# Writing out the loops over chunks of a graph network's steps, and turning a chunk's new states to rows one chunk later

## The reference

```python
h = jnp.maximum(_layernorm(x), 0.0)
# 5 times:
messages = h[col] @ W_msg.T + b_msg
agg = jax.ops.segment_sum(messages, row, num_segments=num_nodes)
gi = agg @ W_ih.T + b_ih
gh = h @ W_hh.T + b_hh
r = sigmoid(i_r + h_r); z = sigmoid(i_z + h_z); n = tanh(i_n + r * h_n)
h = (1.0 - z) * n + z * h
# at the end
return x + h
```

## Time and profile before

| | us |
|---|---|
| runs of the kernel before, median of 2 | 6251.72 (6239.28 to 6264.16) |
| the profiled execution's own time | 6248.37 |
| its span, first to last instruction | 6246.6 |
| first gather of the steps issued (the steps begin) | 1097.0 |

### The profile page before, as it was taken

How to read it: one execution, slowest core, us unless ns; L and a number is a source line. 1 busy time by engine, 2 the same in 40 slices (tenths; PEclk the granted TensorE clock), 3 DMA queues, 4 the chain that set the end, 5 groups by cost and what they waited for, 6 DMA issues and landing times.

```text
span 6246.6 us, 261732 instructions
## 1 busy us (share of the span) xinstructions
PE 4820.9 (77%) x112184; PEld 3776.4 (60%) x112185; DVE 3473.5 (56%) x6216; ACT 3188.3 (51%) x6141; POOL 236.3 (4%) x254
## 2 busy tenths in 40 slices
PE   3664777788888877778888888888788887777777
PEld 1423665666666666666666666666666666666665
DVE  6998777455555554545555555555555554444444
ACT  6202777555555554545455555555555554444444
POOL 0000000000000000000000000000000000000000
PEclk8987888999999999999999999999999999999998
DMA  2002443333333332323323233333233333333332
GB/s 71 2 1 74 163 164 159 113 99 96 101 95 104 102 93 91 102 93 97 97 92 103 92 104 97 100 102 100 95 104 95 100 103 98 97 97 97 97 97 75
DMA packets 227296, 603.16 MB, mean 97 GB/s; under 512 B 23316, under 2 KB 143425, under 8 KB 225966
## 3 DMA queue, kind: packets, MB, share of 16 engines
q1 hardware_dynamic: 217950, 566.55, 27.4%
q0 software_dynamic: 8272, 19.43, 1.3%
HBM read 467.05 MB, written 118.84 MB: 94 GB/s over the span
## 4 chain that ended last, share of the span: by engine, by line
PE 65%; issue 16%; DVE 15%; ACT 2%; DMA 1%; DVEq 1%; SPq 0%; ACTq 0%; POOL 0%
PE f_ps_c L783 21%; PE f_ps_b L769 12%; PE f_ps_a L769 11%; PE f_ps_d L729 3%; PE f_ps_d L816 3%; PE f_ps_d L810 2%; PE f_ps_d L811 2%; PE f_ps_d L812 2%; DVE f_ring L979 2%; PE f_ps_c L803 2%; PE f_ps_d L817 2%; PE f_ps_d L818 2%; PE f_ps_c L823 2%; DVE f_ring L1118 2%; DVE f_hr L1123 1%
## 5 line engine op out<-in xcount | busy, mean ns | idle before, releaser
L783 PE MATMUL f_ps_c<-f_ring 128*32 128x256 f16 x49000 | 2595.7, 281 | 242.5 <-issue 200.5
L588 ACT CAST f_ring<-f_ps_b 128x512 f16<-128x512 f32 x2082 | 1185.0, 588 | 1299.8 <-PE f_ps_b L769 1293.8
L588 ACT CAST f_ring<-f_ps_a 128x512 f16<-128x512 f32 x2083 | 1191.2, 588 | 1157.8 <-PE f_ps_a L769 1151.6
L783 PEld LDWEIGHTS f_ps_c<-f_ring 128*32 128x32 fp8e4 x49000 | 1365.1, 99 | 473.5 <-issue 386.6
L769 PE MATMUL f_ps_b<-f_hr,f_ring 128*32 128x256 f16 x24496 | 1334.9, 281 | 286.1 <-issue 285.0
L769 PE MATMUL f_ps_a<-f_hr,f_ring 128*32 128x256 f16 x24504 | 1297.8, 282 | 200.0 <-issue 190.2
L1151 DVE CAST f_ring<-f_ps_b 128x512 f16<-128x512 f32 x980 | 673.4, 687 | 1085.0 <-PE f_ps_b L769 1084.3
L1151 DVE CAST f_ring<-f_ps_a 128x512 f16<-128x512 f32 x980 | 673.4, 687 | 932.3 <-PE f_ps_a L769 931.8
L769 PEld LDWEIGHTS f_ps_b<-f_hr,f_ring 128*32 128x32 fp8e4 x24496 | 682.7, 99 | 459.8 <-issue 441.0
L769 PEld LDWEIGHTS f_ps_a<-f_hr,f_ring 128*32 128x32 fp8e4 x24504 | 676.6, 99 | 358.8 <-issue 339.3
L508 POOL DMA_INDIRECT f_ring<-fast_hrows,f_idx_tab x245 | 231.1, 943 | 5927.0 <-PE f_ps_c L793 4588.3
(11 more groups left out here) (257 smaller groups left out, 5431.1 us busy)
## 6 DMA issues: line engine op xcount, KB each, us to landing
f_ring<-fast_adj_e SPq DMA_DIRECT2D x245, 800.0 KB, 4.6
f_ring<-fast_adj_o SPq DMA_DIRECT2D x245, 800.0 KB, 6.2
fast_adj_o<-f_ring SPq DMA_DIRECT2D x49, 800.0 KB, 3.4
fast_adj_e<-f_ring SPq DMA_DIRECT2D x49, 800.0 KB, 3.4
f_ring<-fast_deg SPq DMA_DIRECT2D x245, 128.0 KB, 6.2
fast_hrows<-f_hr SPq DMA_DIRECT2D x196, 128.0 KB, 1.8
fast_hrows<-f_hr SPq DMA_DIRECT2D x1, 6272.0 KB, 24.6
f_ring<-in_x_dram SPq DMA_DIRECT2D x48, 128.0 KB, 6.3
```

The lines of the kernel that those rows point to most:

```text
L588: nc.scalar.copy(Gx[b], X[b]).then_inc(evac_a, 1)
L783: pe.matmul(R[ph % 2][32 * j:32 * j + 32, u * CW:(u + 1) * CW], lhsT=o[:, k * P + 32 * j:k * P + 32 * j + 32], rhs=kept[:, u * CW:(u + 1) ...
```

## The change

`run_step` loses its loop: all 49 chunks of a step are written out on PE, ACT and DVE, so that all numbers of chunks and all values of waits are constants. The three `sem_inc` on `pe_turns` go. `turn_rows` of a chunk moves from group 21 of the chunk behind it to group 0 of the next but one: chunk n's group 0 now turns chunk n - 2, into `R[ph % 2]`, the same bank as before. `new_rows` and `add_x` move alike, into a function `finish` at the head of DVE's chunk n, ahead of its first copy. The last chunk of a step is excepted: it is turned at group 21 of the next step's first chunk, and finished at DVE's group 19, as before.

```diff
-        def run_step(eng, s, body):
-            body(s, 0, 0)
-            with eng.Fori(0, (NCH - 1) // 4) as i:
-                for base in range(1, 5):
-                    body(s, base, i)
+        def run_step(s, body):
+            for c in range(NCH):
+                body(s, c, 0)
...
# in place, place_spilled and ahead of a chunk's first expand
-                    pe.sem_inc(pe_turns, 1)
...
# PE's groups
-                        if begun and g == 21:
+                        if g == 0 and (base > 1 or (base == 0 and s > 0)):
+                            turn_rows(m - 1, R[ph % 2])
+                        if g == 21 and base == 0 and s > 0:
                             turn_rows(m, r)
...
# after PE's last step
                 m, ph = TOTAL - 1, (TOTAL - 1) % RING
+                turn_rows(m - 1, R[(m - 1) % 2])
...
# DVE
+                def finish(m, c, s):
+                    if s < STEPS - 1:
+                        new_rows(m, c, s, R[m % 2])
+                    else:
+                        add_x(m, 16 * (c // 2) + 16, c % 2, R[m % 2])
...
+                    if base > 1:
+                        finish(n - 2, base - 2, s)
+                    elif base == 0 and s > 0:
+                        finish(n - 2, NCH - 2, s - 1)
                     for g in DVE_G:
                         evacuate(n, ph, g)
...
                         if g == 19:
                             new_h(m)
-                            if sp_ < STEPS - 1:
-                                new_rows(m, cp, sp_, r)
-                            else:
-                                add_x(m, i * 32 + ((base - 1) // 2 * 16 + 16), (base - 1) % 2, r)
+                            if base == 0:
+                                finish(m, cp, sp_)
...
# after DVE's last step
+                finish(m - 1, c - 1, STEPS - 1)
```

More of the change, by code:

```diff
@@ L621, in _ @@
                 for s in range(STEPS):
-                    run_step(act, s, body)
+                    run_step(s, body)
                 gate_r(TOTAL - 1)
@@ L860, in _ @@
                 for s in range(STEPS):
-                    run_step(pe, s, body)
+                    run_step(s, body)
                 m, ph = TOTAL - 1, (TOTAL - 1) % RING
+                turn_rows(m - 1, R[(m - 1) % 2])
                 for g in range(NG - LAG, NG):
@@ L1240, in body @@
                             new_h(m)
-                            if sp_ < STEPS - 1:
-                                new_rows(m, cp, sp_, r)
-                            else:
-                                add_x(m, i * 32 + ((base - 1) // 2 * 16 + 16), (base - 1) % 2, r)
+                            if base == 0:
+                                finish(m, cp, sp_)
                 for s in range(STEPS):
-                    run_step(dve, s, body)
+                    run_step(s, body)
                 m, c = TOTAL - 1, NCH - 1
                 r = R[m % 2]
+                finish(m - 1, c - 1, STEPS - 1)
                 add_parts(m, r)
```

## The result

| | us |
|---|---|
| after, median of 2 runs | 5072.52 (5071.69 to 5073.36) |
| before, median of 2 runs | 6251.72 (6239.28 to 6264.16) |
| ratio, 95% interval | 0.8114 [0.8044, 0.8183] |
| the profiled execution's span, after | 5070.9 |

A forecast was written before the change was run, and what follows sets the result against it. PE's program was taken to set the pace, with stops for packets of code. From the 6246.6 us span, 312 for the loop's end and 245 for straight chunks came off: 5690 us, range 5480 to 5860.

The forecast's parts named there:

- PE is paced by the bringing of its code: PE's 675.7 us of stops ahead of expand and place matmuls were read as waiting for the next 256-instruction packet of code.
- Fewer instructions on PE: In each chunk 904 instructions fall to 852; at 5.4 us a packet, a straight chunk goes from 19.2 to 18.1 us.
- The loop's end: At PE's 60 loop ends, branch, second stop and slow clock cost 5.2 us each; removing them gains 312 us.
- The moved turn: PE's wait at the turn of the rows for DVE's last product goes, 0.66 us a chunk.
- The cover: Behind the turn, 1.7 us of PE groups hide DVE's finish, 0.5 us to spare; failing would cost 120 us.
- The two gains in the straight chunk don't add up: In straight chunks, fewer packets (1.1 us) and the vanished wait (0.66) overlap; 1.0 us a chunk taken, 245 us in all.
- Straight code streams: PE's stops in the body come from the loop's refetching and go without branches: 4930 us, or 5430 if half go; chance 0.16.
- Both other rivals: Either only PE's branch gain shows, 5935 us (5860 to 6120), chance 0.11; or written-out code is brought more slowly, chance 0.07.
- Slower: Written-out code comes more slowly than a loop's at PE's packet ends; 6935 us at 7 us a packet; chance 0.07.
- The Trainium skill: Its rule that crossing code blocks is mostly hidden was said to disagree with PE's 0.88 and 1.83 us stops in straight code.

The follow-up runs named there:

- the loops' trend: Kernel before with loops of 16 or 24 chunks in place of 4: 6043.04 and 6019.9 us, 4.2 to 4.3 us for each loop end that went.

## Why the prediction was wrong in size and right in direction

- **PE is paced by the bringing of its code: right.** 585.6 of the 675.7 us of stops went, and in the third step the clock went from 0.96 to 1.00. Both traces show it, and the runs with increments put the stops back at will. One step to it came out by luck: the earlier trace rows divides the bytes of queue q8 by the instructions of all engines, but q8 carries PE's code alone. After, its 880 packets of 256 are 225,280 instructions, and PE has 225,181 in the trace. Before, PE ran 238,152, and 1022 packets are 261,632: the surplus, which no kernel without loops has, is code brought around the loop's ends. That a packet holds 256 rests on the stops, which fall on one number modulo 256.
- **The step that failed: "Fewer instructions on PE", where it says that "Beside full code they cost nothing" and "Their price is the code that must be brought".** The count was right (852 a chunk said, 851 there; 3.33 packets, 816 in the steps). The price was not: by packets it was 19.2 - 18.1 = 1.1 us a chunk, 270 us; the increments alone were worth 876 us, or 626 with nothing waiting on them. An increment costs PE little as work; where it stands early in a packet, the next packet's transfer starts later (1.72 to 2.53 us behind the entry in place of 1.13), and PE stops for it. The price of a packet, 5.4 us, was so no constant: now it is 16.0 / 3.33 = 4.8 us, and a chunk without a stop takes 15.56 us against the 15.1 that the prediction had as the floor.
- **The loop's end: 312 us said, 4.2 to 4.3 us each measured, some 255 us.** The intervals of gathers took it 20% too high. Alone, writing out gave 47 us, since the form with constants was dearer as long as the increments stood in it, for a cause that is open. The prediction had no term for that.
- **The moved turn: right.** 0.66 us a chunk said, 0.74 measured without the increments and 0.98 with them; the wait fell to 8.0 us. The cover held: `finish` at DVE's chunk head delays nobody that counts (DVE waits there itself, see below, and `place` waits 3.9 us in all for DVE's copies).

```profile
DVE f_hr L1198 <- PE f_ps_c L819: 142.3, 196, 1.2
```

- **"The two gains in the straight chunk don't add up": wrong.** The move gave 182 us where the stops were gone, and 241 beside full stops, which were to swallow most of it.
- **The first rival, "Straight code streams", came nearest:** 4930 us if all stops go, and its sign, gathers 16 us apart, is what came. It had a chance of 0.16, for the wrong reason: it put the stops down to the branch. Without the branch and with the increments they stay (5948.86 us). "Against it" the prediction said that the stops lie many packets behind the branch; that was right, and meant that something in the straight code made them. The semaphore instructions of the earlier trace rows stood there and were charged for their bytes alone.
- Both other rivals fell: the time is 5072.52 us, below the first's 5860 to 6120, and nothing is slower. But with the increments in it, written-out code was dearer than the loops' trend by some 210 us, the way that "Slower" had it.
- **The Trainium skill.** The prediction says that the first half of the rule "disagrees with rows 4"; meant is the earlier trace rows. The Trainium skill, "Runtime: NRT & Kernel Launch", Instruction fetch mechanics, has the crossing into the next block mostly hidden. The kernel after agrees: 90.1 us of stops over some 816 packets, 0.11 us each. The kernel before doesn't, and the increments make up most of the difference (701.0 us of stops with them and no loop).

In order of the experiments the gain is 6237 - 6190 = 47 us for the loops, 241 for the move and 876 for the increments, 1164 in all. Another order would share it out otherwise: the move is worth 182 when it comes last.

## What to carry to other kernels

This was shown on PE alone. Where it runs through long straight code, a stop at every packet's end asks two things: how long a packet's work is, and how soon in it the next one starts to come. Look at what the sequencer does in the packet's first instructions, and first for semaphore operations that nobody needs. Before charging an instruction by its duration or its bytes, take it out (or put it back) alone; one edit told more here than the whole sum.

## What was not expected of the hardware

- Increments of 51 ns on PE's sequencer cost 118 ns of the kernel's time each, on average, where some four stand in the first 64 instructions of every 256-instruction packet (353 us / 2984), and some 5 ns in the middle (15 / 2988, not clear of the spread of runs).
- The next packet's transfer starts a median of 1.13 us after PE enters a packet where no increment stands early, 1.72 with some four of them there, 2.53 with the increments ahead of all groups; in the stops shown PE goes on 2.0 to 2.5 us after the transfer's start.
- Code that is due during the loads of the 800 KB tables comes later (1.8 us behind the entry in place of 1.1, medians of the kernel after); without the loads the kernel before took 330 us less.
- Left open: why the written-out form with constants cost some 210 us while the increments were there, and why the price of increments doesn't go by the number of early ones. A loop without the increments wasn't tried.
